# A four-layer graph network on one core: product and mask instructions of the first layer for two slots or items each, and the softmax of five probabilities ahead of the edge list

## What is computed

```python
xt = jnp.einsum('ni,tio->tno', x, W)                       # 4 edge types
xj = xt[et, src].reshape(-1, H, C)                         # H = 4 heads, C = 32
xi = xt[et, dst].reshape(-1, H, C)
scores = leaky_relu(jnp.einsum('ehd,khd->ehk', concat([xi, xj]), att_vectors), 0.2)
pk = jax.nn.softmax(confounder_probs)                      # 5 probabilities
alpha = jnp.einsum('ehk,k->eh', scores, pk)
a = exp(alpha - segment_max(alpha, et * N + dst)[seg])     # softmax over the edges of one
alpha_n = a / segment_sum(a, seg)[seg]                     # type that arrive at one node
msg = xj * alpha_n * edge_importance[et]
out = segment_sum(msg, dst) + x @ W[0] + bias
```

## Time and profile before

| | us |
|---|---|
| median of 3 runs | 9856.31 |
| the three runs | 9853.96, 9856.31, 9918.93 |
| the profiled execution, its own time | 9892.94 |
| its span, first to last instruction | 9891.2 |
| outside the span | 1.7 |

### The profile page before, as it was taken

One profiled execution on the slowest core, in us unless ns is written; L12 is line 12 of the kernel. 1 busy time (PEld: TensorE's weight loads), 2 busy tenths in 40 slices (PEclk: granted clock), 3 DMA queues, 4 the chain that ended last, 5 costly groups with the idle time before them and its releaser, 6 DMA issues. The chain is left out here.

```text
span 9891.2 us, 83332 instructions
## 1 busy us (share of the span) xinstructions
PE 4460.2 (45%) x14438; PEld 2760.1 (28%) x14438; DVE 5073.3 (51%) x11750; ACT 1673.0 (17%) x3458; POOL 5779.6 (58%) x5435
## 2 busy tenths in 40 slices
PE   6266676762333332222232222366666666554442
PEld 5122232232222222212121121233333333343332
DVE  7266676674555544544544444444444444554443
ACT  1322222231111111111111111211111111110002
POOL 2455555525655545555555555455556555888886
PEclk8688888875555565555565555677778777765555
DMA  2422222234332323333233333344444444444444
GB/s 59 134 51 51 52 53 54 53 40 132 90 87 79 85 69 83 87 83 89 78 89 84 88 84 83 97 127 126 133 131 134 127 125 51 36 36 36 36 36 85
DMA packets 673823, 804.66 MB, mean 81 GB/s; under 512 B 312241, under 2 KB 513273, under 8 KB 672600
## 3 DMA queue, kind: packets, MB, share of 16 engines
q0 software_dynamic: 317520, 531.92, 26.6%
q1 hardware_dynamic: 313896, 114.11, 4.5%
q10 hardware_dynamic: 42336, 157.90, 4.5%
HBM read 578.06 MB, written 225.40 MB: 81 GB/s over the span
## 5 line engine op out<-in xcount | busy, mean ns | idle before, releaser
L1716 POOL DMA_INDIRECT big<-table_layer,slot_rows_L x2400 | 2298.3, 958 | 1726.5 <-issue 1138.5
L2449 POOL DMA_INDIRECT sums_by_source<-big,to x800 | 1261.3, 1577 | 282.2 <-issue 202.8
L986 POOL DMA_INDIRECT big<-table_layer,idx_L x912 | 931.7, 1022 | 767.0 <-DVE h L1160 442.1
L1735 PE MATMUL own_ps_L<-of_tile_L,big 50*128 50x16 f32 x1224 | 283.1, 369 | 2327.1 <-DVE fade_L L1850 1406.0
L2017 POOL DMA_INDIRECT big<-table_layer,rec_m x904 | 866.8, 959 | 275.4 <-issue 270.5
L2109 DVE SCALAR_TENSOR_TENSOR big<-ps,nbb,big 128x128 f32 x1792 | 545.8, 346 | 923.6 <-remote 592.6
L2048 PE MATMUL ps<-big,w 128*128 128x512 f32 x1792 | 914.3, 658 | 135.5 <-ACT big L2069 103.8
L1735 PEld LDWEIGHTS own_ps_L<-of_tile_L,big 50*128 50x128 f32 x1224 | 271.3, 324 | 2406.0 <-issue 2397.6
L1727 PE MATMUL psH_L<-w,h 128*128 128x256 f32 x1584 | 676.3, 606 | 462.2 <-ACT big L1797 385.1
L1078 PE MATMUL sums_L<-h,ident 128*128 128x512 f32 x1344 | 706.1, 674 | 322.1 <-issue 165.4
L1872 DVE TENSOR_TENSOR_SCAN big<-h,products_L 128x1122 f32<-128x1122 f32 x300 | 747.5, 2492 | 25.4 <-issue 1.0
(11 more groups left out here) (445 smaller groups left out, 7361.0 us busy)
## 6 DMA issues: line engine op xcount, KB each, us to landing
hidden_edge_parts<-big ACTq DMA_DIRECT2D x72, 768.0 KB
hidden_edge_parts<-big ACTq DMA_DIRECT2D x72, 640.0 KB
big<-table_layer,slot_rows_L POOLq DMA_INDIRECT x2400
h<-in_edges ACTq DMA_DIRECT2D x75, 384.0 KB
h<-in_edges ACTq DMA_DIRECT2D x75, 320.0 KB
table_layer<-xr SPq DMA_DIRECT2D x49, 298.0 KB
big<-table_layer,idx_L POOLq DMA_INDIRECT x912
big<-table_layer,rec_m POOLq DMA_INDIRECT x904
```

The costliest lines, as they stand in the source:

```text
L986: G.indirect_dma_start(out=g[b][:, u, s, :], out_offset=None, in_=table, in_offset=bass.IndirectOffsetOnAxis(ap=at, axis=0)).then_inc(gath ...
L1716: G.indirect_dma_start(out=ring[b][:, s, :], out_offset=None, in_=tab1_d[l], in_offset=bass.IndirectOffsetOnAxis(ap=at_rows[b][:, s, R_POS ...
L1735: last = PE.matmul(own_ps[:, c * SLOTS:(c + 1) * SLOTS], own1T[:, c * P:(c + 1) * P], of_tile[b % 2][:, :], start=True, stop=True)
L2449: G.indirect_dma_start(out=sum_d[s], out_offset=bass.IndirectOffsetOnAxis(ap=to[u][:, s:s + 1], axis=0), in_=msg[u][:, s, :], in_offset=No ...
```

## The change

Three parts. In `weigh`, for the first layer, one product instruction takes two slots. In `scores`, for the first layer, one addition of own parts and masks takes two items. In the preparation, the five probabilities are loaded ahead of the edge list under a semaphore of their own, and DVE takes their softmax ahead of the edge list's split; the weight arrays under `w_in` are then 13, and DVE no longer waits for them.

```diff
@@ sync
+                sp.dma_start(soft[:, :], probs.partition_broadcast(P)).then_inc(probs_in, 16)
                 sp.dma_start(e32[:, :], dst).then_inc(edges_in, 16)
...
-                                (bias[:, 1:4, :], bias1.partition_broadcast(P)), (bias1T[:, :], bias1cols),
-                                (soft[:, :], probs.partition_broadcast(P))):
+                                (bias[:, 1:4, :], bias1.partition_broadcast(P)), (bias1T[:, :], bias1cols)):
@@ gpsimd and tensor
-                pool.wait_ge(w_in, 16 * 14)
+                pool.wait_ge(w_in, 16 * 13)
...
-                pe.wait_ge(w_in, 16 * 14)
+                pe.wait_ge(w_in, 16 * 13)
@@ vector, preparation
+                dve.wait_ge(probs_in, 16)
+                V.tensor_reduce(tot[:, 0:1], soft[:, :], AX.X, ALU.max)
...
+                V.tensor_scalar(soft[:, :], soft[:, :], tot[:, 2:3], None, ALU.mult).then_inc(soft_ok, 1)
                 dve.wait_ge(edges_in, 16)
...
-                dve.wait_ge(w_in, 16 * 14)
-                V.tensor_reduce(tot[:, 0:1], soft[:, :], AX.X, ALU.max)
...
-                V.tensor_scalar(soft[:, :], soft[:, :], tot[:, 2:3], None, ALU.mult).then_inc(soft_ok, 1)
                 dve.wait_ge(cst2, NCONST)
@@ vector, scores
-                            for u in range(B):
-                                V.tensor_tensor(zt[:, u, :, :].rearrange("p s (t w) -> p s t w", t=T),
-                                                bc(ob[b][:, u, :].rearrange("p (t w) -> p t w", t=T), 1, S),
-                                                bc(mask[b][:, u * S:(u + 1) * S, :], 3, ZW), ALU.add)
+                            for u in range(0, B, 2):
+                                V.tensor_tensor(
+                                    zt[:, u:u + 2, :, :].rearrange("p u s (t w) -> p u s t w", t=T),
+                                    bc(ob[b][:, u:u + 2, :].rearrange("p u (t w) -> p u t w", t=T), 2, S),
+                                    bc(mask[b][:, u * S:(u + 2) * S, :].rearrange("p (u s) t -> p u s t", s=S), 4, ZW), ALU.add)
@@ vector, weigh
-                            for s in range(S):
+                            for s in range(0, S, 2):
+                                two = slice(s, s + 2)
                                 last = V.tensor_tensor(
-                                    prod[PROD[u]][:, s, :].rearrange("p (t h c) -> p t h c", t=T, h=H),
-                                    bc(w[:, s, :].rearrange("p (t h) -> p t h", t=T), 3, C),
-                                    bc(g[b][:, u, s, 0:D].rearrange("p (h c) -> p h c", h=H), 1, T), ALU.mult)
+                                    prod[PROD[u]][:, two, :].rearrange("p s (t h c) -> p s t h c", t=T, h=H),
+                                    bc(w[:, two, :].rearrange("p s (t h) -> p s t h", t=T), 4, C),
+                                    bc(g[b][:, u, two, 0:D].rearrange("p s (h c) -> p s h c", h=H), 2, T), ALU.mult)
```

More of the change, by code:

```diff
@@ L278, in gnn @@
             w_in = sem("weights_in")
+            probs_in = sem("probs_in")
             x_in = sem("features_in")
@@ L484, in _ @@
                 V.tensor_scalar(soft[:, :], soft[:, :], tot[:, 2:3], None, ALU.mult).then_inc(soft_ok, 1)
+                dve.wait_ge(edges_in, 16)
+                V.tensor_scalar(part[0][:, :], e32[:, :], P - 1, None, ALU.bitwise_and)
+                V.tensor_scalar(part[1][:, :], e32[:, :], 7, None, ALU.arith_shift_right)
+                dve.drain()
+                V.tensor_copy(lo[:, :], part[0][:, :])
+                V.tensor_copy(hi[:, :], part[1][:, :])
+                dve.drain()
                 dve.wait_ge(cst2, NCONST)
```

## The result

| | before | after |
|---|---|---|
| median, same chip, us | 9885.68 (5 runs, 9853.96 to 9918.93) | 9614.78 (5 runs, 9599.79 to 9671.43) |
| profiled execution, its span, us | 9891.2 | 9669.7 |

The ratio is 0.9736, 95% interval 0.9705 to 0.9768: faster by 2.6%; between the two medians lie 271 us. The forecast was 9894, its range 9810 to 9990. It was wrong in sign and in range, and the case that came true is the one that had 0.07.

What follows compares the result with a forecast made beforehand. It took the first-layer loop as a ring of waits, POOL's gather run plus the chain behind it, no engine full. Terms -8 (item 0's products), +52 (waiting gathers), -6 (start) gave +38 on 9856: 9894 us, range 9810 to 9990.

Steps and rivals of the forecast that it cites:

- The ring: First-layer loop, 29.6 us a batch: POOL's 16 gathers (20.36 us), then 9.39 idle until ACT's release, `weights` and item 0's products.
- Item 0's products, -8: First-layer loop: only item 0's two product pairs shorten the path, 0.14 us a batch, 8 us in 56 batches.
- Waits of gathers, 2.2 us a batch: First-layer loop: gathers wait behind longer DVE instructions, so POOL's run of 16 grows by 2.2 us.
- What a batch does that turns over: First-layer loop: late first gathers leave ACT unheld; about half of 28 single-run batches would change to the second form.
- the 14 batches that change over: First-layer batches expected to go from single runs of 16 gathers to pairs, at +0.5 us each, 7 us.
- pairs: First-layer loop, second form: two batches in 61.6 us with one run of 28 gathers; 28 batches already so, +0.5 each.
- +52 us: Gather waits in the first-layer loop: 31 us from 14 batches, 7 from 14 changing over, 14 from 28 in pairs.
- The start, -6: Softmax ahead of the edge list, before the first layer: PE's count starts earlier, gain 6 us, range 1.5 to 10.2.
- A slower POOL loosens the ring: Rival, chance 0.07: most first-layer batches run at 26.3 us, 185 us gone, 9660 us.
- First form stays: Rival, chance 0.26: ACT still held, POOL's run ends 2.2 us later in each first-layer batch, +115 us, 9971 us.
- What would show it: Signs in the first-layer loop: longer gathers, mean above 1.02 us by 0.1 or more, runs of 16 taking 22.6 us.

Runs made afterwards that it cites:

- h1: Kernel before plus one POOL drain a batch ahead of item 2's gathers, vector instructions untouched: 9615.53 us against 9838.03, ratio 0.9782.
- h3: Kernel before with the two-slot products in item 0 alone, where the kernel before takes 9838.03 us: 9813.91 us, ratio 0.9976.
- f1: The whole change against the kernel before, where that takes 8214.06 us and nothing is held: 8354.67 us, ratio 1.0171.
- e7: Kernel before with the two-slot products in item 0 alone, where the kernel before takes 8212.91 us: 8219.19 us, ratio 1.0011.

## Why the prediction was wrong

- **The ring.** Right for the held condition: POOL's run, then a chain behind its end, with ACT released by that end. What I didn't see is that the ring has a way out. h1 shows that a stop of 3 us inside POOL's run releases ACT too, not only the stop at its end.
- **Item 0's products, -8.** h3 gave -24 with an interval of 0.0 to -0.5%, up to 46 us, which takes in -8. That the savings on the chain are small was right.
- **Waits of gathers, 2.2 us a batch.** The mechanism was right, and the single waits to 0.01 us. The sum was short: the mean grew by 0.178 us, 16 x 0.178 = 2.8 us a batch, and f1 has 24.76 - 22.2 = 2.6 us a batch in its time. This misses by 0.6 us a batch, 34 us, and isn't why the forecast failed.
- **What a batch does that turns over: the step that failed.** I wrote that the 14 batches that change over "at +0.5" would join pairs at 30.0 us each, and that pairs stay as they are. I had the observation, that at 640.04 a gather 4.5 us late leaves ACT unheld, and took the 11.7 us of idle time behind its run of 28 as belonging to the form. It is a hold of its own, in the pair's second batch, as ACT's rows in the kernel before show:

```profile
664.92 0.23 ACT L1016 ACTIVATE slots_L<-rec_L 128x32 uint16 x1 [2.68 <-issue]
685.23 0.23 ACT L1024 ACTIVATE big<-run_z_L 128x16 f32 x1 [20.08 <-issue]
```

In these 20 us ACT has only register instructions, loads of its registers and drains to do. They take some 0.7 us each (one 1.41) until 684.7, 4.4 us after the end of POOL's run at 680.26, and less than 0.1 us from there. With waits in every batch this hardly comes: stops of over 5 us fell from 42 to 3, and the batch to 24.9. The term for these batches was thus not +52 us but, with the savings, -259.
- **The start, -6.** The end at 10.2 was right: 443.11 to 433.01 is 10.1 us. The Trainium skill's section "SBUF: two separate sides" ("SBUF — State Buffer") has two SBUF inputs collide only with a GpSimd instruction that reads SBUF, and the trace agrees: 1.09 us at 10.47, inside a blanking of 15.90.
- **The rivals.** "A slower POOL loosens the ring" was the mechanism, with the earlier trace rows as its evidence, four batches of 26.3 us. Its price came out larger than 185 us, since the batch went below 26.3, to POOL's own pace. Its chance of 0.07 was my error, and an avoidable one: the forecast itself rested on late gathers that free ACT, and this rival is only that observation carried to every batch. "First form stays" (+115) has the sum that fits the kernel where nothing is held, +141 with the change. Its condition, a held ACT, is the opposite, so this agreement is luck.
- **What would show it.** "I am wrong if ... it grows and `weights` still follow each other in 29.6 us or less" is what happened.

Left open: what makes the held condition; why ACT is released only when POOL stops, where its gathers follow each other without a pause; and how waits of 1 us or memsets of 0.74, which don't release it in that way, loosen the hold all the same. That instructions reach the sequencers slowly is a reading of the 0.7 us register instructions, not shown; that they come with POOL's runs is. Whether POOL's stops must come before ACT's wait, or anywhere in the run, wasn't separated either.

## What to carry to other kernels

Where an engine is released within a few us of the end of another engine's burst, and the releaser isn't an instruction, ask what happens if the burst is interrupted, before you ask what happens if it gets longer; a late start in the timeline that is followed by an unheld batch is that experiment, already made. Then the slower version of a busy engine can be the faster kernel. And a gain that comes from such a hold belongs to the condition in which it was measured: compare with the kernel before on the same chip in the same minutes, and look at one profile of each kind, since here the same edit gave -2.6% and +1.7%.

## What the runs showed of the hardware

- The kernel before takes some 8213 or some 9850 us, and two chips were met in both conditions. Register instructions of 0.7 us on SP and ACT are found in the longer profiles alone (359 of 2489 against none of 2502 in e7). Held, they get few only with strong spacing of the gathers: 327 with one drain a batch, 221 with the two-slot products, 78 with the change, 71 with two drains, none with a drain behind each gather. They belong to POOL's runs of gathers: of 2681 that wait for nothing in the loop before, plain arithmetic counted in, 374 take that long. 330 of these start during a run, none less than 4 us into it, and 44 in the 5 us behind its end, where none of the 608 that start later is among them. Their number doesn't set the time: with one drain it is nearly that of before, and the batch is 4.6 us shorter.
- A drain on POOL behind a gather costs 2.6 to 2.8 us between two gathers (2.94 us of idle time instead of 0.30), an elementwise memset of 928 values 0.74.
- A blanking on POOL stretched DVE's operation on five numbers from 0.34 to 13.40 us (line 478 of each kernel) and left two-input one-hot instructions at 1.09. Beside this blanking the form of the DVE instruction decided, not its size: 5 elements were held, 1792 were not.
